# Attention in steps of four score tiles: one run of sixteen weighting groups per step

## The chip, the cores and the metric

One Trainium2 chip, of which one core runs the whole program. The number that counts is the device time of one execution in microseconds (us), lower is better. The core has TensorE (PE, with its weight loads listed apart as PEld), VectorE (DVE), ScalarE (ACT), GpSimd (POOL) and SyncE (SP), which issues nearly all transfers. Each engine takes its instructions in the order in which the program gives them, and engines wait for one another through semaphores.

## The reference

The program is a chain of four residual blocks on x (2, 512, 1024): cross attention, a low-rank feed-forward, a quantised product, and a mixing of four streams. The change touches the first alone:

```python
query = q @ w_q.T; key = k @ w_k.T; value = v @ w_v.T      # 32 heads of 32; 8 key/value groups, 4 heads each
scores = jnp.einsum('bghnd,bgsd->bghns', query, key) / D_HEAD ** 0.5
scores = jnp.where(mask, scores, jnp.finfo(scores.dtype).min)
attention = jax.nn.softmax(scores, axis=-1)
out = jnp.einsum('bghns,bgsd->bghnd', attention, value)
```

There are 2 batches x 8 groups = 16 pairs of batch and group. In each there are 4 heads and 512 queries against 1024 keys.

## The kernel before

`stage_b` (line 658) computes the attention. Its unit of work is a **score tile**: one head, 128 queries, 1024 keys. A pair of batch and group has STEPS = 16 tiles (4 blocks of queries x 4 heads), and all 16 pairs have 256. The body of the loop on each engine covers two pairs, 32 tiles, k = 0 to 31; the first and the last body are written out, six run in a loop.

A tile k passes through these stations:

- `score` (L744, PE): two matmuls of 512 columns into psS[k % 2], so psS holds two tiles. The precision is kept by splitting queries and keys into two parts that lie in the 128 rows.
- `mask_min` (L865, DVE): adds the mask and writes the result to Sc, with the minimum of each row to `mins` (a second small instruction reads the accumulator). It frees psS[k % 2] and counts `masked`.
- `exponentials` (L820, ACT): the exponential into Pr, with the row's sum. It counts `probs`.
- `turn` (L780, PE): eight 128x128 transposes into psT, which is single. Its first half may be overwritten when ACT has copied it (`kept[0]`), the second half when DVE has (`kept[1]`).
- `keep`: ACT copies the first half of psT to PT (L828), DVE the second (L874). PT holds two units of eight tiles.
- `weigh` (L758, PE): for a unit of UNIT = 8 tiles (two blocks of queries x four heads), eight groups of four matmuls of 256 columns, each into its own 32 partitions of psO. Each is executed as two instructions, so the call for one tile is 8 rows of PE and 8 of PEld. They work on the unit before the one whose tiles are being turned, so tiles 0 to 7 of the kernel have no weighting beside them. The last unit is weighed by `LastUnit.weigh` (L622).
- once per pair: `reciprocals` (L879, DVE), `keep_O` (L834, ACT), `spread_rec` (L770, PE: 16 small matmuls, 32 rows, directly after a run of weighting), and `normalise` (L886, DVE, after the copy of tile j = 13 of the next pair).

The orders around the change are written out by hand. PE takes two tiles in a step, k0 and k0 + 1:

```python
wait masked k0;   score(k0 + 2)
wait masked k0+1; score(k0 + 3)
turn(k0); weigh(k0); weigh(k0 + 1)
turn(k0 + 1)
```

DVE takes, for each k, `mask_min(k + 2)` and then `keep(k)`; ACT takes `exponentials(k + 1)` and then `keep(k)`. Neither order is touched. SP loads queries, keys and values of the pair after next, when `scored` shows that all 16 tiles of this pair have been scored, and the values when `weighed` shows its units weighed.

Of the kernel before, what the change touches and what calls it, by code (L numbers as in the profile page):

```python
# [657 lines left out]
def stage_b(nc, ident, hand, QHd, QLd, KHd, KLd, Vd, AOd, early, start_early_loads, end):  # L658
# [4 lines left out]
    with ExitStack() as stack:  # L663
# [3 lines left out]
        def sem(name):  # L667
            return stack.enter_context(nc.semaphore(name))

        STEPS = QT * HPG  # L670
        BODY = 2 * STEPS
        UNIT = 2 * HPG
# [26 lines left out]
        masked = sem("b_masked")  # L699
# [10 lines left out]
        @block.sync  # L710
        def _(sp):
            def store(bg, u):
                sp.wait_ge(AO_ready, bg + 1)
                sp.dma_start(AOd[ds(bg, 1)].rearrange("a p q -> p (a q)"), AOs[:, u, :]).then_inc(stored[u], 16)


            start_early_loads(sp)
            for u in range(2):
                sp.wait_ge(hand.stored[u], 32 * (KT + B * KVT))
                sp.wait_ge(hand.q2_stored[u], 16 * NK)  # L720
            sp.wait_ge(hand.v_stored, 16 * B)
            with sp.Fori(0, BG // 2 - 1) as it:
                for u in range(2):
                    sp.wait_ge(scored, it * BODY + (u + 1) * STEPS)
                    hand.load_scores(sp, QHd, QLd, KHd, KLd, it * 2 + (u + 2), u)
                    sp.wait_ge(weighed, (it * 2 + (u + 1)) * (STEPS // UNIT))
                    hand.load_values(sp, Vd, it * 2 + (u + 2), u)
                    store(it * 2 + u, u)
            sp.wait_ge(stored[0], 16 * (GROUPS // 2))
            sp.wait_ge(stored[1], 16 * (GROUPS // 2) + 16)  # L730
            for t in range(2):
                early.load_attention(sp, AOd, t)
            store(BG - 2, 0)

        @block.tensor
        def _(pe):
            def score(it, k):

                u, j = divmod(k, STEPS)
                qt, h = divmod(j, HPG)  # L740
                if j == 0:
                    pe.wait_ge(qkv_in[u], (it + 1) * (16 * QKV_DMAS))
                for n in range(2):
                    last = pe.matmul(psS[:, k % 2, n * HALF:(n + 1) * HALF], Qs[:, u, h, qt * P:(qt + 1) * P],  # L744
                                     Ks[:, u, n * HALF:(n + 1) * HALF], start=True, stop=True)
                last.then_inc(scored, 1)

            def weigh(it, k, first=False):

                u, unit, kt = (k // UNIT - 1) // 2 % 2, k // UNIT - 1, k % UNIT  # L750
                if kt == 0:
                    pe.wait_ge(kept[0], it * BODY + k)
                    pe.wait_ge(kept[1], it * BODY + k)
                    if unit % 2 == 0 and not first:
                        pe.wait_ge(AO_ready, it * 2 + (u - 1))
                cols = slice(unit % 2 * UQ, (unit % 2 + 1) * UQ)
                for h in range(HPG):
                    last = pe.matmul(psO[h * DH:(h + 1) * DH, u, cols], Vs[:, u, kt, :], PT[:, unit % 2, kt, h, :],  # L758
                                     start=(kt == 0), stop=(kt == NK - 1))
                if kt == NK - 1:  # L760
                    last.then_inc(weighed, 1)

            def spread_rec(bg, u):

                pe.wait_ge(rec_ready, bg + 1)
                pe.wait_ge(O_kept, bg + 1)
                for qt in range(QT):
                    for h in range(HPG):
                        one = rec[:, u, qt * HPG + h:qt * HPG + h + 1].to_broadcast([P, DH])
                        last = pe.matmul(psO[h * DH:(h + 1) * DH, u, qt * P:(qt + 1) * P], one, ident[:],  # L770
                                         start=True, stop=True)
                last.then_inc(spread, 1)

            def turn(it, k, first):
                pe.wait_ge(probs, it * BODY + (k + 1))
                for f in range(2):
                    if not (first and k == 0):
                        pe.wait_ge(kept[f], it * BODY + k)
                    for kt in range(NK)[PARTS[f]]:
                        last_t = pe.transpose(psT[:, kt, :], Pr[:, k % PR, kt * P:(kt + 1) * P], ident[:])  # L780
                    last_t.then_inc(turned[f], 1)

            def body(it, first=False, last=False):
                for k0 in range(0, BODY, 2):
                    u, j = divmod(k0, STEPS)
                    if not (last and k0 + 2 >= BODY):
                        for k in (k0, k0 + 1):
                            pe.wait_ge(masked, it * BODY + (k + 1))
                            if k + 2 < BODY:
                                score(it, k + 2)  # L790
                            else:
                                score(it + 1, k + 2 - BODY)
                    turn(it, k0, first)
                    if not (first and k0 < UNIT):
                        for k in (k0, k0 + 1):
                            weigh(it, k, first)
                    if j == UNIT + 2 and not (first and u == 0):
                        spread_rec(it * 2 + (u - 1), 1 - u)
                    turn(it, k0 + 1, first)

            score(0, 0)
            score(0, 1)
            body(0, first=True)
            with pe.Fori(1, BG // 2 - 1) as it:
                body(it)
            body(BG // 2 - 1, last=True)

        @block.scalar
# [1378 lines left out]
```

## Time and profile before

| | |
|---|---|
| Median of the runs | 1158.68 us |
| Runs | 1156.39, 1158.68 and 2424.54 us |
| The profiled execution | 1156.01 us |
| Its span, first to last instruction | 1154.2 us |
| Granted TensorE clock over the span | 0.96 |
| PE / PEld busy | 1048.2 us (91%) / 787.1 us (68%) |
| DVE / ACT busy | 862.3 us (75%) / 663.2 us (57%) |
| First score matmul to last normalise of stage B | 211.0 to 732.8 us |

How to read it: the span is that of one profiled execution, and sums are made against that one. Ends of matmuls are modelled, so a PE that is busy in every slice need not be at its peak; the distance between the starts of two instructions is the safer measure. The shares of busy time are means over stages with different limits. In the rows, "x8" is a merged group of eight instructions in order, and a bracket gives the idle time of the engine before the group and what ended it.

### The profile page before, as it was taken

The numbers are of one execution on the slowest core, as the hardware profiler recorded it, in microseconds if no ns is written. First come the engines' busy times: TensorE is split into PE (matmuls) and PEld (weight loads), VectorE is DVE, ScalarE is ACT, GpSimd is POOL, SyncE is SP. The second block draws the span as 40 slices with busy tenths as digits, with TensorE's granted clock in tenths as the row PEclk, the third lists the DMA queues.
The fourth block names the chain that finished last, engine by engine and source line by source line (L and its number), as shares of the span: only waits on it lengthen the run. The fifth ranks groups of instructions, "written<-read, shape, count | busy, mean of one in ns | idle before, by whom it ended". The sixth has DMA issues, their size and how long they took to land. (4 is left out here: it accounts for less than half of the span.)

```text
span 1154.2 us, 21362 instructions
## 1 busy us (share of the span) xinstructions
PE 1048.2 (91%) x7552; PEld 787.1 (68%) x7552; DVE 862.3 (75%) x1888; ACT 663.2 (57%) x1125; POOL 91.9 (8%) x75
## 2 busy tenths in 40 slices
PE   6999998799999999999999999989999977669518
PEld 5878887577777777777777777758888843446217
DVE  5854434799999999999999999647543336679998
ACT  4422211598888898988888888422221156436215
POOL 1210103100000000000000000000112034500000
PEclk9999999899999999999999999989999989879859
DMA  8368877622221122222222210753130000000003
GB/s 339 135 210 289 293 205 267 258 57 70 70 60 42 47 61 68 68 68 65 67 68 68 52 46 23 280 164 110 55 146 0 0 14 1 0 1 1 1 0 146
DMA packets 55569, 112.95 MB, mean 98 GB/s; under 512 B 7725, under 2 KB 21165, under 8 KB 55389
## 3 DMA queue, kind: packets, MB, share of 16 engines
q1 hardware_dynamic: 55452, 112.26, 31.3%
q8 instruction: 32, 0.52, 0.2%
q14 instruction: 21, 0.16, 0.0%
q0 software_dynamic: 64, 0.00, 0.0%
HBM read 83.99 MB, written 27.26 MB: 96 GB/s over the span
## 5 line engine op out<-in xcount | busy, mean ns | idle before, releaser
L865 DVE CUSTOM_DVE_ANT_0 XS<-b_psS,b_mbias 128x1024 f32<-128x1024 f32 x256 | 311.1, 1215 | 0.9 <-PE b_psS L744 0.7
L820 ACT ACTIVATE XS<-XS,b_mins 128x1024 f32<-128x1024 f32 x256 | 295.5, 1154 | 10.9 <-DVE b_mins L865 10.4
L780 PEld LDWEIGHTS b_psT<-ident,XS 128*128 128x128 f32 x2048 | 230.7, 141 | 68.8 <-issue 50.5
L780 PE MATMUL b_psT<-ident,XS 128*128 128x128 f32 x2048 | 274.4, 277 | 1.3 <-ACT b_PT L828 1.3
L874 DVE COPY b_PT<-b_psT 128x512 f32<-128x512 f32 x256 | 176.9, 691 | 34.7 <-PE b_psT L780 33.1
L828 ACT COPY b_PT<-b_psT 128x512 f32<-128x512 f32 x256 | 149.4, 584 | 46.8 <-PE b_psT L780 38.3
L744 PE MATMUL b_psS<-XTh 128*128 128x512 f32 x512 | 157.8, 426 | 6.7 <-PEq L102 5.5
L758 PE MATMUL b_psO<-b_PT,XTh 128*32 128x256 f32 x1984 | 132.8, 385 | 0.0
L744 PEld LDWEIGHTS b_psS<-XTh 128*128 128x128 f32 x512 | 86.1, 191 | 25.6 <-DVE b_mins L865 9.3
L758 PEld LDWEIGHTS b_psO<-b_PT,XTh 128*32 128x32 f32 x1984 | 51.8, 109 | 42.1 <-issue 20.8
L1213 ACT ACTIVATE c_sd<-c_mv,c_eps 128x1 f32<-128x1 f32 x16 | 4.7, 295 | 104.6 <-DVE c_mv L1303 104.6
L1842 PE MATMUL e_psT<-e_XN,e_dg 128*128 x128 | 29.7, 396 | 38.6 <-DVE XR L2075 38.6
L399 ACT ACTIVATE a_oh<-a_psM 128x512 fp32r<-128x512 f32 x24 | 14.2, 596 | 84.1 <-PE a_psM L322 50.7
L1296 DVE TENSOR_TENSOR XR<-XR,c_psM 128x1024 f32<-128x1024 f32 (+1 forms) x16 | 19.5, 1218 | 56.9 <-PE c_psM L1118 56.9
L480 DVE SCALAR_TENSOR_TENSOR a_ol<-a_psM,a_oh 128x512 fp32r<-128x512 f32 x24 | 16.5, 690 | 53.4 <-ACT a_oh L399 53.3
L1842 PEld LDWEIGHTS e_psT<-e_XN,e_dg 128*128 128x128 f32 x128 | 25.5, 200 | 43.2 <-issue 39.5
L1118 PE MATMUL c_psM<-WEh,c_Lh 128*128 128x512 f32 x128 | 51.1, 400 | 0.0
L322 PE MATMUL a_psM<-XTh,WTl 128*128 128x512 f32 x128 | 50.8, 397 | 0.0
L322 PE MATMUL a_psM<-XTh,WTh 128*128 128x512 f32 x128 | 50.7, 396 | 0.0
L1118 PE MATMUL c_psM<-WEh,c_Ll 128*128 128x512 f32 x128 | 50.6, 395 | 0.0
L1118 PE MATMUL c_psM<-WEl,c_Lh 128*128 128x512 f32 x128 | 50.6, 395 | 0.0
L322 PE MATMUL a_psM<-XTl,WTh 128*128 128x512 f32 x128 | 49.9, 390 | 0.0
(236 smaller groups left out, 1642.0 us busy)
## 6 DMA issues: line engine op xcount, KB each, us to landing
XS<-in_ctx SPq DMA_DIRECT2D x16, 512.0 KB, 5.7
XTh<-QHd SPq DMA_DIRECT2D x32, 256.0 KB, 4.7
XTh<-QLd SPq DMA_DIRECT2D x32, 256.0 KB, 5.3
XS<-in_ctx_turned SPq DMA_DIRECT2D x8, 512.0 KB, 9.4
XS<-in_x SPq DMA_DIRECT2D x8, 512.0 KB, 10.4
a_wst<-in_L_xattn_w_q SPq DMA_DIRECT2D x8, 512.0 KB, 5.7
a_xn<-in_ctx_turned SPq DMA_DIRECT2D x8, 512.0 KB, 4.2
QHd<-a_oh SPq DMA_DIRECT2D x16, 256.0 KB, 5.5
```

What stands on the lines that cost most here:

```text
L322: last = pe.matmul(psM[:, m % 4, :], a[:, w % 2, k, :], b[:, k, cols], start=(k == 0 and a is WTh and b is mh), stop=(k == KT - 1 and a is ...
L480: dve.scalar_tensor_tensor(out=ol[:, m % 2, :], in0=psM[:, m % 4, :], scalar=inv_root if M_Q <= m < M_V1 else 1.0, in1=oh[:, m % 2, :].bit ...
L744: last = pe.matmul(psS[:, k % 2, n * HALF:(n + 1) * HALF], Qs[:, u, h, qt * P:(qt + 1) * P], Ks[:, u, n * HALF:(n + 1) * HALF], start=True ...
L758: last = pe.matmul(psO[h * DH:(h + 1) * DH, u, cols], Vs[:, u, kt, :], PT[:, unit % 2, kt, h, :], start=(kt == 0), stop=(kt == NK - 1))
L780: last_t = pe.transpose(psT[:, kt, :], Pr[:, k % PR, kt * P:(kt + 1) * P], ident[:])
L820: act.activation(Pr[:, k % PR, :], Sc[:, k % 4, :], ACT.Exp, bias=mins[:, k % 4:k % 4 + 1], scale=-1.0, accum_out=sums[:, u, j:j + 1]).the ...
L828: act.copy(PT[:, (k // UNIT) % 2, PARTS[0], k % HPG, queries(k)], psT[:, PARTS[0], :]).then_inc(kept[0], 1)
L865: dve.tensor_tensor_reduce(out=Sc[:, k % 4, :], in0=psS[:, k % 2, :], in1=mbias[:, qt, :], scale=1.0, scalar=3.4e38, op0=ALU.add, op1=ALU.min,
L874: dve.tensor_copy(PT[:, (k // UNIT) % 2, PARTS[1], k % HPG, queries(k)], psT[:, PARTS[1], :]).then_inc(kept[1], 1)
L1118: last = pe.matmul(psM[:, u, cols], a[:, u, k, :], w[:, k, cols], start=(k == 0 and i == 0), stop=(k == KT - 1 and i == 2))
L1296: dve.tensor_tensor(row, row, psM[:, u, :], ALU.add).then_inc(added, 1)
L1842: last = pe.matmul(psX(u)[:, i * CH:(i + 1) * CH], dg[:, u, n, i, :], XN[:, ds(t, 1), n * CH:(n + 1) * CH].rearrange("p a n -> p (a n)"), ...
```

## The change

PE's body takes four tiles in a step. The calls of `weigh` for the four stand in one run after the first transposition, where before there were two runs of two. `score` runs for tiles k0 + 4 and k0 + 5 after the second transposition, for k0 + 6 after the third and for k0 + 7 after the fourth; before, they ran in pairs after the second and after the fourth. The rule for the wait is the same: tile k is scored once tile k - 2 is masked. Tiles 2 and 3 are scored ahead of the first body. `spread_rec` comes after the run of weighting at j = 12, before at j = 10. No instruction is added or removed, and no other engine's program is changed.

```diff
+            def score_next(it, k, last):
+
+                if k < BODY:
+                    pe.wait_ge(masked, it * BODY + (k - 1))
+                    score(it, k)
+                elif not last:
+                    pe.wait_ge(masked, it * BODY + (k - 1))
+                    score(it + 1, k - BODY)
+
             def body(it, first=False, last=False):
-                for k0 in range(0, BODY, 2):
+                for k0 in range(0, BODY, 4):
                     u, j = divmod(k0, STEPS)
-                    if not (last and k0 + 2 >= BODY):
-                        for k in (k0, k0 + 1):
-                            pe.wait_ge(masked, it * BODY + (k + 1))
-                            if k + 2 < BODY:
-                                score(it, k + 2)
-                            else:
-                                score(it + 1, k + 2 - BODY)
                     turn(it, k0, first)
                     if not (first and k0 < UNIT):
-                        for k in (k0, k0 + 1):
+                        for k in range(k0, k0 + 4):
                             weigh(it, k, first)
-                    if j == UNIT + 2 and not (first and u == 0):
+                    if j == UNIT + 4 and not (first and u == 0):
                         spread_rec(it * 2 + (u - 1), 1 - u)
                     turn(it, k0 + 1, first)
+                    score_next(it, k0 + 4, last)
+                    score_next(it, k0 + 5, last)
+                    turn(it, k0 + 2, first)
+                    score_next(it, k0 + 6, last)
+                    turn(it, k0 + 3, first)
+                    score_next(it, k0 + 7, last)
 
             score(0, 0)
             score(0, 1)
+            for k in (2, 3):
+                pe.wait_ge(masked, k - 1)
+                score(0, k)
             body(0, first=True)
```

## Rows read from the trace of the kernel before

**Rows 1.** Windows, transpositions' stretch: PE, PEld, DVE, ACT, POOL busy, PEclk, DMA, GB/s

```profile
215.90:722.40 506.50, 505.14 (x5016) 376.07 (x5015) 471.87 (x793) 450.58 (x780) 0.00 (x0) 1.00 0.26 66
```

**Rows 2.** Who waited for whom in stage B: total us, times, longest

```profile
PEld b_psT L780 <- issue: 50.5, 130, 0.5
ACT b_PT L828 <- PE b_psT L780: 38.3, 101, 1.3
DVE b_PT L874 <- PE b_psT L780: 33.1, 90, 1.5
PEld b_psO L758 <- issue: 20.8, 124, 0.2
PEld b_psS L744 <- DVE b_mins L865: 9.3, 20, 1.8
```

**Rows 3.** Timeline of an undisturbed pair of tiles: start, us, engine, line, instruction

```profile
567.02 1.09 PE L780 MATMUL b_psT<-ident,XS 128*128 128x128 f32 x8
567.87 1.18 PE L744 MATMUL b_psS<-XTh 128*128 128x512 f32 x4
568.15 0.69 DVE L874 COPY b_PT<-b_psT 128x512 f32<-128x512 f32 x1
568.80 1.23 DVE L865 CUSTOM_DVE_ANT_0 XS<-b_psS,b_mbias 128x1024 f32<-128x1024 f32 x1
568.89 1.04 PE L780 MATMUL b_psT<-ident,XS 128*128 128x128 f32 x8
569.96 0.69 DVE L874 COPY b_PT<-b_psT 128x512 f32<-128x512 f32 x1
570.57 1.22 DVE L865 CUSTOM_DVE_ANT_0 XS<-b_psS,b_mbias 128x1024 f32<-128x1024 f32 x1
570.85 1.09 PE L780 MATMUL b_psT<-ident,XS 128*128 128x128 f32 x8
571.98 0.69 DVE L874 COPY b_PT<-b_psT 128x512 f32<-128x512 f32 x1 [0.19 <-PE b_psT L780]
```

**Rows 4.** Timeline where a score waits for the mask of two tiles earlier

```profile
562.73 1.15 ACT L820 ACTIVATE XS<-XS,b_mins 128x1024 f32<-128x1024 f32 x1 [0.50 <-DVE b_mins L865]
564.35 0.08 DVE L865 DVE_READ_ACCUMULATOR2_ANT b_mins<- 128x1 f32 x1
564.49 0.30 PEld L744 LDWEIGHTS b_psS<-XTh 128*128 128x128 f32 x2 [0.38 <-DVE b_mins L865]
565.05 1.04 PE L780 MATMUL b_psT<-ident,XS 128*128 128x128 f32 x8
```

**Rows 5.** Timeline where the spreading of the reciprocals lengthens a run of weighting

```profile
393.28 1.04 PE L780 MATMUL b_psT<-ident,XS 128*128 128x128 f32 x8
396.12 1.09 PE L780 MATMUL b_psT<-ident,XS 128*128 128x128 f32 x8
397.26 0.69 DVE L874 COPY b_PT<-b_psT 128x512 f32<-128x512 f32 x1 [1.07 <-PE b_psT L780]
```

**Rows 6.** Timeline of the last unit, weighed in one run, and one matmul's length (tile b_psO)

```profile
724.17 3.66 PE L622 MATMUL b_psO<-b_PT,XTh 128*32 128x256 f32 x64 [1.37 <-PEq L663]
...
L758 PE MATMUL b_psO<-b_PT,XTh x1984: 379/379/403, 232.4 to 721.4; 128*32 128x256 f32 x199
```

**Rows 7.** Timeline around a normalisation on DVE

```profile
560.87 0.68 DVE L886 TENSOR_TENSOR b_AOs<-b_psO,b_Os 128x512 f32<-128x512 f32 x1
561.47 1.22 DVE L865 CUSTOM_DVE_ANT_0 XS<-b_psS,b_mbias 128x1024 f32<-128x1024 f32 x1
```

**Rows 8.** DVE's copies and normalisations, first and last start (tiles b_psT, b_psO)

```profile
L874 DVE COPY b_PT<-b_psT x256: 685/692/694, 218.2 to 722.8; 128x512 f32<-128x512 f32 x128
...
L886 DVE TENSOR_TENSOR b_AOs<-b_psO,b_Os x15: 680/681/681, 274.4 to 720.0; 128x512 f32<-128x512 f32 x15
```

**Rows 9.** Timeline: weight loads on both sides of a run of weighting

```profile
569.85 0.59 PEld L758 LDWEIGHTS b_psO<-b_PT,XTh 128*32 128x32 f32 x16 [0.17 <-issue]
...
570.85 0.86 PEld L780 LDWEIGHTS b_psT<-ident,XS 128*128 128x128 f32 x8 [0.41 <-issue]
```

## The prediction

> **What bounds the kernel now.** I read the windows first. Between the first and the last transposition PE is busy 505.14 of 506.50 us at the full clock of 2.4 GHz (granted 1.00), DVE 471.87 and ACT 450.58 [rows 1]. Ends of matmuls are modelled, so "busy" is no proof. The table of waits says more: DVE and ACT sit idle for PE's transpositions (33.1 and 38.3 us), PE waits for DVE 9.3 us in all [rows 2]. The timeline shows the pace. From one transposition to the one two tiles later it is 570.85 - 567.02 = 3.83 us, with no gap on PE, and DVE's idle 0.19 us ends when the transposition is done [rows 3]. So PE sets the pace at 7.66 us for four tiles. DVE is close behind: copy to mask 0.61 (569.96 to 570.57; 0.65 the other time), mask to next copy 1.16, 1.77 us a tile, 7.08 for four.
>
> **The part that gains.** First PE alone, by distances of starts [rows 3]. A transposition to the next thing is 567.87 - 567.02 = 0.85. Two tiles of scores take 1.02 (567.87 to 568.89). A run of weighting of two tiles takes 1.96 - 0.85 = 1.11 (568.89 to 570.85). The last unit gives the pace inside such a run: 64 instructions, 3.66 us, less one matmul's 0.38, over 15 distances of four instructions, is 0.219 per four [rows 6], so 16 instructions are 0.875 and going in and out of a run costs 1.11 - 0.875 = 0.235. A step of four tiles has one such run fewer: -0.235. A single tile's scores take 565.05 - 564.49 = 0.56 [rows 4], so two singles in place of a pair cost 2 x 0.56 - 1.02 = +0.10. PE's own work falls from 7.66 to **7.53** us a step.
>
> A rule speaks for a larger gain. Rows first: PEld idles 0.17 us before a run of weighting and 0.41 after it [rows 9]. The Trainium skill (TensorEngine Tiling (Array Packing), section Key Properties) says that changing the tiling mode drains TensorE; the trace agrees in that both idle times stand where full-width and 32-column instructions meet. Were the whole idle the price, a switch less would save 0.58; by starts it is 0.235, because the matmuls ahead are still streaming in that time. The sum goes by 0.235.
>
> **The part that costs.** Call the step's tiles 0 to 3. The distance from transposition 0 to transposition 1 becomes 1.96 + 0.875 = 2.84 us, since the whole run stands there. The trace has this case already: the spreading stretches one run so that the distance is 396.12 - 393.28 = 2.84, and DVE idles 1.07 us [rows 5]. After it, PE would have to catch up by sending transpositions faster than DVE's 1.77, at 0.85 + 0.56 = 1.41 for the last two. It can't, because score k waits for mask k - 2, and DVE makes mask k + 2 right before copy k. Before, every second score of a pair was tied so closely; now the score of tile 6 after transposition 2 waits for mask 4, and that of tile 7 after transposition 3 for mask 5. Queued behind each waiting score is the next transposition, which DVE and ACT wait for.
>
> The ledger of one step, us from the start of transposition 1, with distances from rows 3 and 4: transposition to DVE's copy 1.13 (567.02 to 568.15), mask start to its accumulator's end 1.23 (568.80 + 1.23 = 570.03), from there to the waiting score's weight load 0.06 (564.35 + 0.08 = 564.43 to 564.49), then 0.56 to the next transposition.
> - Copy 1 at 1.13, mask 4 at 1.74, done 2.97 (score 4, started at 0.85, is long there).
> - Transposition 2 at 1.87 (0.85 + 1.02). PE reaches score 6 at 2.72 and waits till 3.03: stall 0.31. Transposition 3 at 3.59.
> - Copy 2 at 3.00, mask 5 at 3.61, done 4.84; copy 3 at 4.77.
> - PE reaches score 7 at 4.44 and waits till 4.90: stall 0.46. The next transposition 0 is at 5.46, its copy at 6.59, where DVE could have been at 6.54. PE has no lead at all.
> - Transposition 1 again at 5.46 + 2.84 = **8.30**. DVE idles 1.07 before its copy.
>
> Stalls 0.77 + work 7.53 = 8.30, against 7.66: +0.64 a step. The same ledger on the old order gives 1.96 + 1.87 = 3.83 a pair, as in the row. ACT is not in it: where it waits for a mask, its exponential takes 1.15 from there [rows 4], so exponential 4 is done near 4.2 and is needed at 5.46. Weighting runs beside 248 of 256 tiles (1984 instructions, eight a tile [rows 6]), 62 steps: 62 x 0.64 = **+39.7**.
>
> Once per pair of batch and group: the spreading costs PE 2.84 - 1.96 = 0.88 as before, behind a longer run, and stays at that. The normalisation delays the next mask by 0.60 [rows 7], now right on the chain (copy 1, mask 4, score 6). Before, 16 tiles took 504.6 / 255 x 16 = 31.66 [rows 8], less 4 x 7.66 and 0.88 leaves 0.14 for it. So +0.46 x 15 = **+6.9**. The reciprocal falls into DVE's idle 1.07: nothing, and at most its row's length if that idle were gone. SP's queue: the last score of a pair stands where it stood, after its fourth-last transposition, so the loads of queries and keys start as before; the values are released two tiles earlier and the store a little with the normalisation; all have a pair's 30 us of cover. The two scores ahead of the first body wait once for masks they waited for before: nothing.
>
> Sum: +39.7 + 6.9 = +46.6. On the profiled execution, 1156.0, this is 1202.6; the median of the runs lies 2.7 higher, so the forecast is **1205 us**. Unknown sizes: the stall per step is good to 0.15 (the distances in the rows differ by 0.04, and four of them enter), 9 us; the normalisation may cost from nothing to its 0.60, -7 to +2. The forecast's own range is 1189 to 1217. A clock that fell in the stalls is bounded by 0.31 and 0.46 us of waiting; rows with DVE-made waits of 0.38 lie in a stretch granted 1.00 [rows 1, 4], so I take none.
>
> **Rivals.**
> - PE stays the pace (0.12). If the masks are there when PE comes to score them, only PE's work counts: 62 x -0.13 = -8, 1151 us. For it: PE waited for masks only 20 times before [rows 2]. Against: with DVE's order the mask before copy k can't be done earlier than copy k - 1 plus 0.61 + 1.23.
> - The drain rule holds in full and no stall comes (0.06): 62 x -0.58 = -36, 1123 us, faster. For it: 50.5 + 20.8 us of idle weight loads [rows 2], half of it 35.6. Against: the distances of starts, and DVE, whose 34.6 us of idle in the stretch [rows 1] this would use up wholly.
> - The switch is worth 0.58 and the masks bind (0.06): the distance from 0 to 1 is 2.84 - 0.345 = 2.50, the cycle 7.96, +0.30 x 62 + 7 = +25, 1184 us, at the edge of what counts as slower.
> - The change does not lengthen the run (0.01), because the four calls wait inside: their copies are all done by then, since the unit before is finished.
>
> The forecast has 0.75. The side on which it turns is the sum of the last two distances: slower holds as long as transpositions 2 to 4 need more than 7.66 - 2.84 - 1.87 = 2.95 us; PE's work there is 2.82, DVE's pace makes it 3.54 at least.
>
> **The numbers.** The range takes in the forecast's own and the 1184 case from below, and leaves out 1151 and 1123: 1178 to 1218. About 2% (23 us, above 1181.9 or below 1135.5) can be told from no change. Slower: 0.75 and half of 0.06, 0.78. Within: 0.12, half of 0.06 and the 0.01, 0.16. Faster: 0.06.
>
> **What would show it.** In the timeline of the changed kernel: transposition 0 to 1 near 2.84, then 1.87, 1.72 and 1.87, 8.30 for four tiles. In the waits: about 62 times two weight loads of scores that wait for the mask, near 48 us in all where 9.3 stood, and DVE idle for transpositions near 75 in place of 33.1, ACT likewise. PEld's idle "issue" at the transpositions should halve, to near 25. PE's busy time falls, DVE's stays, stage B is 47 us longer and the other stages keep their lengths. Wrong would be a distance 0 to 1 below 2.5, or waits for masks that stay near 9 us.

## The result, and the profile after

The changed kernel takes 1195.2 us (median; 1193.11 to 1198.38), the kernel before beside it 1158.76. The ratio is 1.0329, with a 95% interval of 1.0304 to 1.0353: slower by 36.4 us, where +46.6 was forecast. The ratio is formed from the fast runs alone, without the one of 2424.54 us, so it need not be the quotient of the two medians, 1.0314. The profiled execution took 1193.11 us against 1156.01, +37.1.

The first view is the windows over the same stretch, from the first to the last transposition, with the columns of [rows 1].

```profile
215.90:760.60 544.70, 515.63 (x5016) 384.07 (x5015) 466.53 (x793) 454.53 (x780) 0.00 (x0) 1.00 0.25 61
```

PE, busy all through before, now has 29 us of gaps in 544.70 us (its ends are modelled; distances of starts below say more). DVE does the same work in a stretch 38 us longer. The granted clock is 1.00 over the stretch with these gaps, the upper level of 2.4 GHz. The stage's copies on DVE bound its length:

```profile
L885 DVE COPY b_PT<-b_psT x256: 684/692/693, 218.2 to 761.0; 128x512 f32<-128x512 f32 x128
```

542.8 us from first to last copy, where it was 504.6 [rows 8]: +38.2. From the last copy to the end of the span it is 430.3 us against 431.4, so nothing outside this stage adds to the time. The waits, as in [rows 2], the largest of this stage:

```profile
DVE b_PT L885 <- PE b_psT L780: 77.7, 65, 1.9
ACT b_PT L839 <- PE b_psT L780: 74.8, 64, 2.0
PEld b_psS L744 <- DVE b_mins L876: 61.2, 130, 1.8
PE b_psS L744 <- DVE b_mins L876: 24.0, 92, 1.1
PEld b_psT L780 <- ACT XS L831: 13.9, 33, 0.7
PEld b_psT L780 <- issue: 12.0, 39, 0.5
```

Both sides now wait for each other. DVE idles 77.7 us for transpositions, in 65 waits, about one for each of the 62 steps, and 130 times a score's weight load waits for a mask, about two per step. One step in the timeline (start, us, engine, line, instruction; idle time before it in brackets; other rows between these are left out):

```profile
499.09 1.09 PE L780 MATMUL b_psT<-ident,XS 128*128 128x128 f32 x8
500.22 0.69 DVE L885 COPY b_PT<-b_psT 128x512 f32<-128x512 f32 x1 [1.06 <-PE b_psT L780]
500.86 1.23 DVE L876 CUSTOM_DVE_ANT_0 XS<-b_psS,b_mbias 128x1024 f32<-128x1024 f32 x1
500.94 1.03 PE L780 MATMUL b_psT<-ident,XS 128*128 128x128 f32 x8
502.01 0.08 DVE L876 DVE_READ_ACCUMULATOR2_ANT b_mins<- 128x1 f32 x1
502.02 0.69 DVE L885 COPY b_PT<-b_psT 128x512 f32<-128x512 f32 x1
502.15 0.30 PEld L744 LDWEIGHTS b_psS<-XTh 128*128 128x128 f32 x2 [0.41 <-DVE b_mins L876]
502.72 1.03 PE L780 MATMUL b_psT<-ident,XS 128*128 128x128 f32 x8
503.90 0.30 PEld L744 LDWEIGHTS b_psS<-XTh 128*128 128x128 f32 x2 [0.39 <-DVE b_mins L876]
504.47 1.03 PE L780 MATMUL b_psT<-ident,XS 128*128 128x128 f32 x8
505.43 1.93 PE L758 MATMUL b_psO<-b_PT,XTh 128*32 128x256 f32 x32
507.30 1.09 PE L780 MATMUL b_psT<-ident,XS 128*128 128x128 f32 x8
```

The row at 499.09 is transposition 1. The distances from there are 1.85, 1.78, 1.75 and 2.83 us, 8.21 for four tiles where it was 7.66. DVE has waited 1.06 us for transposition 1, because the whole run of weighting stood ahead of it. After that its work is unbroken: mask 4 ends at 502.09 and the load of score 6 starts 0.06 later; the load of score 7 does the same after mask 5. By starts, PE could have begun score 6 at 500.94 + 0.85 = 501.79 and began it at 502.15, 0.36 us late; score 7 was 0.33 late (503.57 to 503.90).

### The profile page after: what moved, and what is told of

Its sections match the earlier page's. It is cut to its first block and busy times, and to the rows that moved or that the text cites. A ratio compares the mean times of both kernels' runs of the same rounds, so it can differ in the third digit from the quotient of the medians.

```text
span 1191.3 us, 21369 instructions
## 1 busy us (share of the span) xinstructions
PE 1058.7 (89%) x7547; PEld 796.0 (67%) x7552; DVE 858.8 (72%) x1888; ACT 667.0 (56%) x1125; POOL 91.9 (8%) x75
## 5 line engine op out<-in xcount | busy, mean ns | idle before, releaser
L780 PE MATMUL b_psT<-ident,XS 128*128 128x128 f32 x2048 | 270.1, 275 | 1.2 <-ACT b_PT L839 1.2
L780 PEld LDWEIGHTS b_psT<-ident,XS 128*128 128x128 f32 x2048 | 234.5, 141 | 51.5 <-ACT XS L831 13.9
L885 DVE COPY b_PT<-b_psT 128x512 f32<-128x512 f32 x256 | 176.9, 691 | 77.9 <-PE b_psT L780 77.7
L744 PE MATMUL b_psS<-XTh 128*128 128x512 f32 x512 | 171.4, 436 | 34.5 <-DVE b_mins L876 24.0
L744 PEld LDWEIGHTS b_psS<-XTh 128*128 128x128 f32 x512 | 82.1, 190 | 72.9 <-DVE b_mins L876 61.2
L758 PE MATMUL b_psO<-b_PT,XTh 128*32 128x256 f32 x1984 | 119.9, 382 | 0.0
L758 PEld LDWEIGHTS b_psO<-b_PT,XTh 128*32 128x32 f32 x1984 | 58.1, 109 | 42.3 <-issue 10.4
```

The source lines that it names most:

```text
L885: dve.tensor_copy(PT[:, (k // UNIT) % 2, PARTS[1], k % HPG, queries(k)], psT[:, PARTS[1], :]).then_inc(kept[1], 1)
```

## The experiments

The theory: the long run makes one distance between transpositions 2.83 us, and DVE has nothing to do in part of it. The other three together can't be shorter than three of DVE's tiles (mask and copy, 1.77 us each), because psT is single, so that a transposition waits for the copies of the one before, and because score k waits for mask k - 2. PE can't make the lost time good. The main rivals: the spreading of the scores, with its tighter waits, costs the time; a change into or out of a run is dearer than the distances of starts say; the position of PE's work within a step is free. All ratios are to the kernel before. The edits are shown in short form, without their context, and "..." stands for what is left out. They are to the changed kernel, or to the kernel before where a text says so; the two with one tile in each gap are to the kernel before, the second shown against the first.

**One part alone: the merged run, with scores in pairs.**

```diff
-                    score_next(it, k0 + 6, last)
                     turn(it, k0 + 3, first)
+                    score_next(it, k0 + 6, last)
                     score_next(it, k0 + 7, last)
```

> The run of four tiles' weighting stays merged, but the scores go back into pairs (tiles 4 and 5 after transposition 1, tiles 6 and 7 after transposition 3). Theory (the long run leaves DVE idle, and then DVE's own pace of 1.75 us per tile, through the single psT and the two psS, keeps PE from catching up): transposition 3 now follows transposition 2 without a score between, but waits for DVE's copy 2, and score 7 waits for mask 5 as before, so four tiles take about 8.17 us against 8.21 of the changed kernel, and the kernel 1190 to 1196 us. Rival (the spreading of the scores is what costs): with the pairs back only the gain of the merged run is left, 7.43 us for four tiles, about 1145 us.

Measured: 1197.59 us, ratio 1.0344 (1.0314 to 1.0374), a little above the 1190 to 1196 expected. The timeline of PE, one step from transposition 1:

```profile
534.29 1.09 PE L780 MATMUL b_psT<-ident,XS 128*128 128x128 f32 x8
...
536.17 1.04 PE L780 MATMUL b_psT<-ident,XS 128*128 128x128 f32 x8
537.54 1.11 PE L780 MATMUL b_psT<-ident,XS 128*128 128x128 f32 x8 [0.33 <-ACT b_PT L839]
...
539.70 1.03 PE L780 MATMUL b_psT<-ident,XS 128*128 128x128 f32 x8
...
542.53 1.09 PE L780 MATMUL b_psT<-ident,XS 128*128 128x128 f32 x8
```

542.53 - 534.29 = 8.24 us (8.17 expected), in distances of 1.88, 1.37, 2.16 and 2.83. Without score 6 between them, transpositions 2 and 3 meet at the single psT: the wait is for a copy instead of a mask. One distance is 1.37, the next 2.16: it is the three together, 5.41, that DVE holds. The merged run costs the whole loss by itself; the rival's 1145 us is excluded. Spreading the scores gained and lost nothing that shows: the ratios, 1.0329 and 1.0344, lie within each other's intervals.

**The other part alone: scores two, one and one, weighting in two runs.**

```diff
                         for k in range(k0, k0 + 4):          # becomes (k0, k0 + 1)
                             weigh(it, k, first)
...
                     turn(it, k0 + 2, first)
+                    if not (first and k0 < UNIT):
+                        for k in (k0 + 2, k0 + 3):
+                            weigh(it, k, first)
                     score_next(it, k0 + 6, last)
```

> The scores stay spread two, one and one, but the weighting is in two runs of two tiles again (after transpositions 0 and 2). Theory: gaps between transpositions 1.96, 1.87, 2.52 and 1.41 us, PE bound at 7.76 us for four tiles, 0.10 more than before because a score that stands alone costs 0.05 more: before plus 6, about 1165 us, and hardly any wait for masks. Rival (the spreading of the scores costs the 37 us by the tight wait for the mask): about 1195 us.

Measured: 1163.94 us, ratio 1.006 (1.0043 to 1.0078). PE's timeline, every transposition of one step:

```profile
548.12 1.09 PE L780 MATMUL b_psT<-ident,XS 128*128 128x128 f32 x8
...
549.98 1.03 PE L780 MATMUL b_psT<-ident,XS 128*128 128x128 f32 x8
...
552.52 1.04 PE L780 MATMUL b_psT<-ident,XS 128*128 128x128 f32 x8
...
553.89 1.11 PE L780 MATMUL b_psT<-ident,XS 128*128 128x128 f32 x8
...
555.93 1.09 PE L780 MATMUL b_psT<-ident,XS 128*128 128x128 f32 x8
```

7.81 us from 548.12 to 555.93, against the forecast 7.76: the distance of 2.54, which holds a short run and a score, is followed by one of 1.37, and PE catches up. A step so uneven costs next to nothing beyond PE's own 0.10. By the theory's own sum, 2.54 and three of DVE's tiles make 7.85, barely more than the 7.76 of PE alone, so there is next to nothing to make good. The waits say "mask" here as well (21.5 us in all for scores' weight loads), so a wait in that table is not yet a loss.

**The price of a run, first attempt: one tile's weighting and one score in each gap.**

```diff
-                for k0 in range(0, BODY, 2):
+                for k in range(BODY):
                     turn(it, k, first); weigh(it, k, first)   # spread_rec at j == UNIT + 2
                     wait masked k + 1;  score(it, k + 2)
```

> The order before, but one tile's weighting and one tile's score between any two transpositions, so that there are four runs of weighting and four single scores for four tiles, at even distances. It prices the change into and out of a run. Theory: 0.235 us for in and out, 0.05 for each single score: 0.85 + 0.67 + 0.56 = 2.08 us a tile, 8.32 for four, before plus 0.66 x 62 = 41, about 1200 us, with PE never waiting. Rival (a change costs the whole idle of the weight loads, 0.58 us): 2.42 us a tile, before plus 84 or more, about 1243 us.

Measured: 1774.98 us, ratio 1.5322 (1.5276 to 1.5367). Theory and rival both missed, because of how I had built it. The waits:

```profile
ACT XS L817 <- DVE b_mins L862: 687.4, 255, 4.9
DVE XS L862 <- PE b_psS L744: 651.7, 254, 4.8
PEld b_psT L780 <- DVE b_PT L871: 455.3, 254, 2.3
```

With score k + 2 behind transposition k, DVE's mask k + 2 waits for it, copy k stands behind that mask, and transposition k + 1 waits for copy k. All engines take turns. In the kernel before, the score that DVE needs next is always at least one transposition ahead of this. The even distances of this order count for nothing beside that.

**The same, with the score one tile further ahead.**

```diff
-                    wait masked k + 1;  score(it, k + 2)
+                    wait masked k + 2;  score(it, k + 3)      # score 2 also ahead of the first body
```

> One tile's weighting and one tile's score in each gap again, but the score is that of tile k + 3 and no longer that of k + 2, so that DVE's mask k + 2, which stands before its copy k, finds its score done. Theory: this lead is what the earlier kernel with one of each lacked, and now PE runs without a wait: 0.85 + 0.67 + 0.56 = 2.08 us a tile, 8.32 for four, before plus 41, about 1197 us. Rival (going into and out of a run costs the whole idle of the weight loads, 0.58 us): 2.42 us a tile, about 1240 us. If the lead was not the cause: near 1775 us again.

Measured: 1196.34 us, ratio 1.0354 (1.0336 to 1.0372), as expected. PE's timeline, one tile:

```profile
530.99 1.03 PE L780 MATMUL b_psT<-ident,XS 128*128 128x128 f32 x8
...
533.09 1.03 PE L780 MATMUL b_psT<-ident,XS 128*128 128x128 f32 x8
```

2.10 us a tile, against 2.08 forecast and 2.42 by the rival. So going into and out of a run costs about 0.24 us and a lone score 0.05, as read from distances of starts. This settles the question on the drain: of the 0.58 us that the weight loads idle around a run, more than half is not lost. That matmuls already loaded still stream in it is the likely reason; the rows can't show it, since ends are modelled. The run also confirms the missing lead as the cause in the run before.

**Taking DVE's pace away: a narrow mask, on both kernels.**

```diff
-  out=Sc[:, k % 4, :], in0=psS[:, k % 2, :], in1=mbias[:, qt, :]
+  out=Sc[:, k % 4, 0:256], in0=psS[:, k % 2, 0:256], in1=mbias[:, qt, 0:256]
-  act.activation(Pr[:, k % PR, :], Sc[:, k % 4, :], ACT.Exp, ...)
+  act.activation(Pr[...] as 4 x 256, Sc[:, k % 4, 0:256] repeated four times, ACT.Exp, ...)
```

> The kernel before with DVE's mask over 256 of the 1024 columns, and the exponential reading these 256 four times; what is left out is the masking of the other 768 columns, and ACT's and PE's work keep their sizes. DVE is then far from being the bound. Theory: PE's order alone counts, 7.66 us for four tiles as before; only the 0.3 us for the normalisation go, so 1152 to 1158 us.

> The changed kernel with the same narrow mask (768 of 1024 columns left out). Theory: with the mask made in well under half of its time scores 6 and 7 don't wait, PE's own work of 7.53 us for four tiles is all, and the kernel is 0.13 x 62 = 8 us faster than the kernel before with the same narrow mask: about 1147 us. First rival (a change into and out of a run costs 0.58 us): 30 us faster than it, about 1125 us. Second rival (something other than DVE's pace costs the 37 us, as the order on PE or the transfers): still 30 us or more slower than it.

Measured: 1150.77 us (ratio 0.9965, 0.9952 to 0.9978; 1152 to 1158 expected) and 1153.15 us (0.9983, 0.9969 to 0.9997). The mask now takes 0.41 us instead of 1.22. The 37 us are gone: the second rival falls, and what held the changed kernel was DVE's pace. The first rival's 1125 us falls too. But the changed order is not the 8 us faster that were expected: from the first to the last transposition it takes 502.3 us (216.0 to 718.3), the other 502.1 (216.7 to 718.8). The medians differ by 2.4 us, and in the traces next to nothing of that lies in this stretch. Its timeline shows who comes next:

```profile
503.39 1.15 ACT L831 ACTIVATE XS<-XS,b_mins 128x1024 f32<-128x1024 f32 x1
503.64 1.11 PE L780 MATMUL b_psT<-ident,XS 128*128 128x128 f32 x8
504.53 0.57 ACT L840 COPY b_PT<-b_psT 128x512 f32<-128x512 f32 x1
505.22 0.86 PEld L780 LDWEIGHTS b_psT<-ident,XS 128*128 128x128 f32 x8 [0.44 <-issue]
```

The profile calls the wait before the transposition at 505.22 "issue", but its time fits ACT's copy, which ends at 505.10 and could start only when the exponential before it was done. ACT's tile, exponential and copy, takes 1.61 us here (504.53 to the next copy at 506.14), and so does this distance (503.64 to 505.25), where PE alone needs 1.41.

**Taking ACT's away too.**

```diff
-  act.activation(Pr[...] as 4 x 256, Sc[:, k % 4, 0:256] repeated four times, ACT.Exp, ...)
+  act.activation(Pr[:, k % PR, 0:256], Sc[:, k % 4, 0:256], ACT.Exp, ...)
-  pe.transpose(psT[:, kt, :], Pr[:, k % PR, kt * P:(kt + 1) * P], ident[:])
+  pe.transpose(psT[:, kt, :], Pr[:, k % PR, kt % 2 * P:(kt % 2 + 1) * P], ident[:])
```

> The kernel before with DVE's mask and ACT's exponential over 256 of the 1024 columns (the other 768 are left out), while the transpositions read these 256 four times and PE's work keeps its size. Theory: PE alone is the pace, 7.66 us for four tiles, about 1151 us, as with the narrow mask alone.

> The changed kernel with the same two narrow operations. With the narrow mask alone its third and fourth distance were still held by ACT (1.37 and 1.61 us), and the gain of PE's order, 0.13 us in four tiles, did not show. Theory: with ACT out of the way too, PE's own 7.53 us for four tiles are all, and it is 8 us faster than the kernel before with the same two: about 1143 us. Rival (nothing is gained by fewer runs of weighting): the same time, 1151 us.

Measured: 1152.57 us (0.9973, 0.996 to 0.9986) and 1146.46 us (0.9933, 0.991 to 0.9958). Four tiles in the changed order, PE alone:

```profile
535.20 1.09 PE L780 MATMUL b_psT<-ident,XS 128*128 128x128 f32 x8
...
537.06 1.03 PE L780 MATMUL b_psT<-ident,XS 128*128 128x128 f32 x8
...
538.43 1.11 PE L780 MATMUL b_psT<-ident,XS 128*128 128x128 f32 x8
...
539.84 1.13 PE L780 MATMUL b_psT<-ident,XS 128*128 128x128 f32 x8
...
542.77 1.09 PE L780 MATMUL b_psT<-ident,XS 128*128 128x128 f32 x8
```

7.57 us, where the narrow kernel before has 3.85 a pair (536.40 to 540.25), 7.70. From the first to the last transposition it is 495.9 against 501.7 us. The distance that was 1.61 is now 1.41; the one of 1.37, which the expectation also laid to ACT, has not changed. So the gain of the changed order is real, 0.13 us in four tiles and 6 us in all (8 expected), and it showed only with both DVE and ACT well below PE's pace.

**Order within the step: one score moved ahead of the run.**

```diff
                     turn(it, k0, first)
+                    score_next(it, k0 + 4, last)
                     ...run of weighting, turn(it, k0 + 1)...
-                    score_next(it, k0 + 4, last)
                     score_next(it, k0 + 5, last)
```

> The changed kernel with the score of tile 4 ahead of the run of weighting instead of after transposition 1; DVE's order as it is. It lengthens the distance from transposition 0 to 1 by 0.56 us and shortens the next by 0.44. Theory: DVE's three other distances can't go below its pace of 1.75 us, so what is added to the long one is lost whole: 3.39 + 3 x 1.77 = 8.7 us for four tiles, 1191 + 32, about 1225 us. Rival (PE's order may be changed within a step at no cost, since its work is the same): 1195 to 1200 us.

Measured: 1249.15 us, ratio 1.0815 (1.0778 to 1.0852). The rival falls, and the theory was right in sign but short by 24 us. The distances of one step:

```profile
533.48 1.03 PE L780 MATMUL b_psT<-ident,XS 128*128 128x128 f32 x8
...
537.22 1.09 PE L780 MATMUL b_psT<-ident,XS 128*128 128x128 f32 x8
...
538.64 1.11 PE L780 MATMUL b_psT<-ident,XS 128*128 128x128 f32 x8
...
540.80 1.03 PE L780 MATMUL b_psT<-ident,XS 128*128 128x128 f32 x8
...
542.55 1.04 PE L780 MATMUL b_psT<-ident,XS 128*128 128x128 f32 x8
543.84 0.72 PE L744 MATMUL b_psS<-XTh 128*128 128x512 f32 x2 [0.26 <-DVE b_mins L876]
```

1.42, 2.16 and 1.75 us are together as forecast (5.33 for three, 5.31 expected), but the score that now stands ahead of the run waits for its mask too, and the fourth distance is 3.74 (533.48 to 537.22) instead of 3.39. That is 9.07 a step; (9.07 - 7.66) x 62 = 87 us explains the measured 94 nearly. The last two rows are the start of the next step and show the wait that is meant.

**Giving DVE a mask to make during the run.** PE's edit as above, one mask more ahead of the first body, and on DVE:

```diff
-    mask_min(k + 2)
+    if k % 4 == 1: mask_min(k + 2)
+    if k % 4:      mask_min(k + 3)
     keep(k)
```

> The changed kernel with two edits: the score of tile 4 stands ahead of the run of weighting, and DVE makes mask 4 before copy 1, mask 5 before copy 2 and mask 6 before copy 3, so that DVE has a mask to make while the run lasts, and scores 6 and 7 find their masks done. Theory: the waits of scores for masks all but vanish, but two copies (3 and the next 0) now follow each other with no mask between, and with psT single the transposition between them stands bare: four tiles take about 8.33 us, 1195 to 1210 us. Rival (the waits of scores for masks are the whole loss): PE's own work alone, 7.63 us for four tiles, about 1158 us.

Measured: 1203.92 us, ratio 1.0406 (1.038 to 1.0433). The waits of this kernel:

```profile
DVE b_PT L885 <- PE b_psT L780: 85.7, 128, 1.9
PEld b_psT L780 <- DVE b_PT L885: 49.1, 128, 0.8
```

```profile
541.33 1.09 PE L780 MATMUL b_psT<-ident,XS 128*128 128x128 f32 x8
...
549.68 1.09 PE L780 MATMUL b_psT<-ident,XS 128*128 128x128 f32 x8
```

Waits of scores for masks have all but gone (3.5 us on their weight loads), and four tiles take 549.68 - 541.33 = 8.35 us, against 8.33 forecast. The rival's 1158 us falls: the waits for masks were not the whole loss. DVE's idle time is still there, now twice a step: once in the run, once between two copies with no mask between them, where the transposition stands bare. A second psT might hide the run; this is argued only, and was not tried: psS (8 KB a partition), psT and psO (4 KB each) are held all through the stage. Of the orders tried none beats the kernel before.

## Why the prediction was right

**What bounds it.** Right. With far less work on DVE, and then on ACT too, the kernel before gained 0.35% and 0.27% (ratios 0.9965 and 0.9973), so PE's own work was the pace; the changed order showed that DVE stood close behind.

**The gain.** Right in size: 0.13 us in four tiles, shown once both other engines were out of the way (7.70 to 7.57, each 0.04 above the prediction's 7.66 and 7.53). The price of a run, 0.235, holds (2.10 us a tile against 2.08). The Trainium skill (TensorEngine Tiling (Array Packing), section Key Properties) has the drain at a change of tiling mode; the rows agree that going into a run and out of it costs time, and put it at under half of the idle time of the weight loads.

**The long distance.** 2.84 forecast from distances of starts, and found again in the spreading's row [rows 5]; 2.83 measured. DVE's idle: 1.07 forecast, 1.06 measured.

**The stalls.** Right in mechanism, large by 0.09. The ledger had 1.87, 1.72, 1.87 and 2.84, 8.30 in all; the trace has 1.85, 1.78, 1.75 and 2.83, 8.21. The term: I let copy 2 wait for transposition 2 plus 1.13. It started 1.08 after it, right behind mask 4, at DVE's own pace of 1.80 from copy 1, so mask 5 ended 1.75 after mask 4 and not 1.87. The two stalls, forecast as 0.31 and 0.46, were 0.36 and 0.33. That is 62 x 0.09 = 5.6 us of the 9.5 too many.

**The normalisation.** The other term that was mis-sized: +0.46 x 15 was forecast. I took the 16 tiles' mean over the whole stage, which includes the first eight tiles without weighting, and so got 0.14 us for what it cost before. Between two transpositions that follow the spreading there are, in the kernel before and the changed one:

```profile
396.12 1.09 PE L780 MATMUL b_psT<-ident,XS 128*128 128x128 f32 x8
...
427.94 1.09 PE L780 MATMUL b_psT<-ident,XS 128*128 128x128 f32 x8
```

```profile
482.04 1.09 PE L780 MATMUL b_psT<-ident,XS 128*128 128x128 f32 x8
...
516.39 1.09 PE L780 MATMUL b_psT<-ident,XS 128*128 128x128 f32 x8
```

31.82 and 34.35 us. Less four steps and 0.88 for the spreading that leaves 0.30 before and 0.63 after: +0.33, 5 us in all. Both remainders are a little large, because most steps take 7.69 and 8.23 us and not the 7.66 and 8.21 of the ones shown; the distance that holds the normalisation is 2.07 before (562.98 to 565.05, 1.88 without) and 2.31 after (586.89 to 589.20, 1.77 without), 0.19 and 0.54. The difference is the same within 0.02. The sum now reads 62 x 0.55 + 15 x 0.33 = 39.1, against 38.2 measured between first and last copy; 1.1 us comes back behind the stage.

**The signs to look for.** DVE's idle time near 75 (77.7), two waits for masks per step (130 in all), PEld's idle at the transpositions halved to near 25 (12.0 for issue and 13.9 that the profile puts down to ACT; the same 0.41 us ahead of a transposition stands under ACT at 499.08 and under issue at 507.30). The waits for masks were put at 48 us: on PEld they are 61.2, since it could have loaded ahead, on PE 24.0. How far a step exceeds PE's forecast work, 8.21 - 7.53 = 0.68 us, 42 us in all, is the safer number. One sign failed: PE's busy time was to fall, and it rose, from 505.14 to 515.63 us in the stretch. The busy time of the score matmuls alone went from 157.8 to 171.4 us; since ends are modelled, this says little of PE's work, and it should not have been named as a sign.

**The rivals.** PE as the pace all through: excluded by the 130 waits and by the merged run alone. The full price of the drain, with or without the waits for masks: excluded by the one-of-each kernel with its lead. (Without them its price left out the two single scores: with +0.10 it would have been 62 x -0.48 = -30 us and not -36.) A run that is not lengthened: excluded by the distance of 2.83. What was right for the narrow kernels, 6 us of gain, is nearly what the first rival gave for the whole.

## What to carry to other kernels

When one engine is the pace and two others are nearly as busy (93% and 89% here), with a single buffer between them, count the distances between the hand-overs and not the work in a step. A step then costs about its long distance and one follower's tile for each of the others (2.83 + 3 x 1.77 = 8.14 here, 8.21 measured), where that is more than the producer's own work (7.53). Price a switch from distances of starts; the idle time of the weight loads overstates it. Before moving a producer in an in-order queue, ask which consumer stands behind the instruction that waits for it: one tile of lead was worth 579 us here, a part of it by the clock that fell (below).

## What the runs showed of the hardware

The granted clock did not react to short waits on PE: it is 1.00 over the changed kernel's stretch, with PE busy 515.63 of 544.70 us, two scores a step late by 0.36 and 0.33 us and the longest gap 0.7. It is 1.00 too from 240 to 700 us of the kernel with a score ahead of the run, where PE is busy only 413.18 of 460.00 us. In the one-of-each kernel without lead, where PE waits some 1.5 us in every tile (379.2 us in 254 waits for DVE's copy), it did (windows, columns as in [rows 1]):

```profile
600.00:800.00 200.00, 135.49 (x888) 79.25 (x886) 83.02 (x138) 76.12 (x134) 0.00 (x0) 0.79 0.13 29
```

0.79 is a mean of the two levels, 1.2 and 2.4 GHz. Part of that kernel's time is this; how much was not separated.
